# Edge counts of a graph network stored as bfloat16 instead of bytes, and fed to TensorE without a cast

## The reference, cut to what matters

```
# layer 2, a polynomial of degree 5 in the normalised adjacency
for k in range(1, 6):
    tx = segment_sum(norm[:, None] * tx[col], row, num_segments=N)    # norm = dis[row] * dis[col]
    result = result + coeffs[k] * tx
# layer 3, two graph convolutions
h = x @ W
agg = segment_sum(h[src] * (dinv[src] * dinv[dst])[:, None], dst, num_segments=N)
out = agg + h / deg[:, None] + b
```

## Time and profile before

| what | value |
|---|---|
| median of 3 runs | 7933.46 us (7933.38 to 7944.13) |
| profiled execution, its own time | 7934.18 us |
| its span, first to last instruction | 7932.5 us |
| mean granted TensorE clock | 0.964 of full speed |
| busy | PE 6931.4 us (87%), DVE 5980.0 (75%), ACT 4364.6 (55%), POOL 2865.0 (36%) |
| DMA | 1425.59 MB, mean 180 GB/s |
| casts of counts, ACT L1384 | 500 in the polynomial, mean 1475 ns; 200 in the convolutions, mean 1475 ns |
| casts of counts, DVE L1468 | 500, mean 1033 ns; 200, mean 1022 ns |

### The profile page before, as it was taken

One profiled execution on the slowest core, in us unless ns is written; L12 is line 12 of the kernel. 1 busy time (PEld: TensorE's weight loads), 2 busy tenths in 40 slices (PEclk: granted clock), 3 DMA queues, 4 the chain that ended last, 5 costly groups with the idle time before them and its releaser, 6 DMA issues. The chain is left out here.

```text
span 7932.5 us, 279512 instructions
## 1 busy us (share of the span) xinstructions
PE 6931.4 (87%) x98699; PEld 5909.3 (74%) x98724; DVE 5980.0 (75%) x17395; ACT 4364.6 (55%) x13164; POOL 2865.0 (36%) x2957
## 2 busy tenths in 40 slices
PE   2799999999999799999994888888895999998888
PEld 1455555555555599999994787788895998997878
DVE  4567776777767599898996799799898667776556
ACT  0122222222222299999994787787795666665555
POOL 0588888888878655454552000000000000000000
PEclk9999999999999999999997999999998999998889
DMA  9522222222222277676674887887895777764645
GB/s 391 164 59 60 59 61 60 59 59 60 59 60 59 64 230 232 227 230 230 229 231 156 284 298 278 284 298 280 297 334 191 200 201 201 201 195 133 175 136 162
DMA packets 656939, 1425.59 MB, mean 180 GB/s; under 512 B 284864, under 2 KB 352190, under 8 KB 653265
## 3 DMA queue, kind: packets, MB, share of 16 engines
q1 hardware_dynamic: 540674, 1232.57, 48.4%
q0 software_dynamic: 101792, 92.82, 5.6%
q10 hardware_dynamic: 13924, 93.06, 3.1%
HBM read 982.95 MB, written 433.34 MB: 179 GB/s over the span
## 5 line engine op out<-in xcount | busy, mean ns | idle before, releaser
L340 POOL DMA_INDIRECT sorted_rows<-sort_rows,sort_row_at x1600 | 1979.4, 1237 | 579.2 <-issue 565.2
L1603 ACT ACTIVATE smooth_msg<-smooth_ps_a,smooth_w_rows 128x64 f32<-128x64 f32 x6000 | 1311.9, 334 | 315.7 <-PE smooth_ps_a L1689 299.2
L371 ACT ACTIVATE sort_count<-sort_ps_c 50x50 bf16<-50x50 f32 x1600 | 331.7, 207 | 1903.2 <-PE sort_ps_c L403 1903.1
L1384 ACT ACTIVATE poly_cast<-poly_mat 128x1536 bf16<-128x1536 uint8 x500 | 714.8, 1475 | 445.0 <-PE poly_ps L1405 370.2
L399 PEld LDWEIGHTS sort_ps_r<-sort_count,sort_hot_dt 50*125 50x125 bf16 x1600 | 282.7, 177 | 837.1 <-issue 582.4
L413 PE MATMUL sort_ps_m<-sort_w,sort_hidden 128*125 128x64 f32 x3200 | 879.3, 430 | 0.0
L1711 PE MATMUL smooth_ps_s<-smooth_msg,smooth_hot 128*128 128x64 bf16 x7500 | 773.9, 195 | 76.2 <-DVE smooth_last_part L1842 65.4
L392 PE MATMUL sort_ps_h<-sort_attrs,sort_w 24*128 24x500 f32 x800 | 811.6, 1115 | 18.1 <-DMA sort_attrs<-in_attr_t 18.1
L1711 PE MATMUL smooth_ps_s<-smooth_rest,smooth_hot 128*128 128x64 bf16 x7500 | 769.8, 194 | 16.0 <-issue 15.9
L1711 PE MATMUL smooth_ps_s<-smooth_last_part,smooth_hot 128*128 128x64 bf16 x7500 | 768.9, 194 | 16.1 <-issue 16.1
L413 PEld LDWEIGHTS sort_ps_m<-sort_w,sort_hidden 128*125 128x125 f32 x3200 | 732.1, 320 | 41.1
(11 more groups left out here) (332 smaller groups left out, 16527.5 us busy)
## 6 DMA issues: line engine op xcount, KB each, us to landing
poly_mat<-counts_t SPq DMA_DIRECT2D x500, 400.0 KB, 3.7
smooth_src<-src_rows SPq DMA_DIRECT2D x150, 960.0 KB, 5.0
smooth_hot<-hot_rows SPq DMA_DIRECT2D x150, 960.0 KB, 7.0
smooth_src<-src_rows SPq DMA_DIRECT2D x150, 640.0 KB, 5.7
smooth_hot<-hot_rows SPq DMA_DIRECT2D x150, 640.0 KB, 6.9
graph_edges<-sorted_rows SPq DMA_DIRECT2D x125, 700.0 KB
hot_rows<-graph_hot SPq DMA_DIRECT2D x125, 640.0 KB, 3.6
src_rows<-graph_hot_t SPq DMA_DIRECT2D x125, 640.0 KB, 3.4
```

Of the source, the lines that this page charges most:

```text
L340: pool.indirect_dma_start(out=sorted_rows, out_offset=bass.IndirectOffsetOnAxis(row_at[u][:, j:j + 1], 0), in_=rows[u][:, j, :], in_offset ...
L1384: act.activation(cast[u][h][:, DVE_S:HR, :], mat[u][h][:, DVE_S:HR, :], ACT.Copy)\
L1603: last = act.activation(at[:, i, :], ps_a[g % 2][:, i * D:(i + 1) * D], ACT.Copy, scale=w_rows[u][:, c * CHUNK + i:c * CHUNK + i + 1])
```

## The change

`st_c`, `st_t`, `counts` and `counts_t` become bfloat16, so the stores of counts and the loads of `mat` carry twice the bytes (a half of a row is 800 KB). The `cast` tiles, ACT's and DVE's casts and their semaphores go. PE reads `mat` itself and waits for the load's semaphore. SP reloads the first half of a row when PE has done 25 blocks of the row two before it (`half_done`, new), the second when PE has done the row (`row_done`). So two rows of `mat` are all that lies between DRAM and PE. ACT has only `write_table` left in `spread`.

```diff
-        st_c = [sb(f"st_c{b}", [128, 2, S_LOAD, 128], U8) for b in two]
-        st_t = [sb(f"st_t{b}", [128, S_LOAD, 2, 128], U8) for b in two]
+        st_c = [sb(f"st_c{b}", [128, 2, S_LOAD, 128], BF16) for b in two]
+        st_t = [sb(f"st_t{b}", [128, S_LOAD, 2, 128], BF16) for b in two]
...
-        mat = [[sb(f"mat{u}{h}", [128, HR, 128], U8) for h in two] for u in two]
-        cast = [[sb(f"cast{u}{h}", [128, HR, 128], BF16) for h in two] for u in two]
+        mat = [[sb(f"mat{u}{h}", [128, HR, 128], BF16) for h in two] for u in two]
...
-        cast_v, cast_a, row_done, row_kept = (sem(n) for n in ("cast_v", "cast_a", "row_done", "row_kept"))
+        row_done, row_kept = sem("row_done"), sem("row_kept")
+        half_done = sem("half_done")
...
-                                for by in (cast_a, cast_v):
-                                    sp.wait_ge(by, 2 * number(k, p, u) + (h + 1 - 4))
-                                    sp.sem_inc(taken, 1)
+                                sp.wait_ge((half_done, row_done)[h], number(k, p, u) - 1)
+                                sp.sem_inc(taken, 1)
...
-                def pair(k, p):
-                    for u in two:
-                        if not at_start(k, p):
-                            act.wait_ge(row_done, number(k, p, u) - 1)
-                        for h in two:
-                            act.wait_ge(loaded[u][h], k * 16 * PAIRS + 16 * p + 16)
-                            act.activation(cast[u][h][:, DVE_S:HR, :], mat[u][h][:, DVE_S:HR, :], ACT.Copy)\
-                               .then_inc(cast_a, 1)
-
                 for k in range(n_passes):
-                    pair(k, 0)
                     act.wait_ge(posted, PAIRS * (k + 1))
                     spilled.write_table(act, xs)
-                    with act.Fori(1, PAIRS) as p:
-                        pair(k, p)
...
                         if b in (0, HR):
-                            for by in (cast_a, cast_v):
-                                pe.wait_ge(by, 2 * number(k, p, u) + (b // HR + 1))
+                            pe.wait_ge(loaded[u][b // HR], k * 16 * PAIRS + 16 * p + 16)
...
-                        last = nc.tensor.matmul(ps[u][:, 0:3 * D], cast[u][b // HR][0:NL, b % HR, :],
+                        last = nc.tensor.matmul(ps[u][:, 0:3 * D], mat[u][b // HR][0:NL, b % HR, :],
                                                 parts[k % 2][:, b].rearrange("p i d -> p (i d)"),
                                                 start=b == 0, stop=b == NB - 1 and not own_edges)
+                        if b == HR - 1:
+                            last.then_inc(half_done, 1)
...
-                def cast_half(k, p, u, h):
-                    dve.wait_ge(loaded[u][h], k * 16 * PAIRS + 16 * p + 16)
-                    dve.tensor_copy(cast[u][h][:, 0:DVE_S, :], mat[u][h][:, 0:DVE_S, :]).then_inc(cast_v, 1)
-
...
-    counts = dram("counts", [NB, 128, NB, 128], U8)
-    counts_t = dram("counts_t", [NB, 128, NB, 128], U8)
+    counts = dram("counts", [NB, 128, NB, 128], BF16)
+    counts_t = dram("counts_t", [NB, 128, NB, 128], BF16)
```

More of the change, by code:

```diff
@@ L1322, in spread @@
     HR = NB // 2
-    DVE_S = 13
     SPILL_AT, LATE, TWICE = 2, 6, 20
@@ L1476, in pair @@
                         for h in two:
[L1477 to L1480, removed]
                             by_row[u].go(at_once)
@@ L1485, in pair @@
                     ahead.end()
-                for u in two:
-                    for h in two:
-                        cast_half(0, 0, u, h)
                 none = Beside(iter(()))
```

## The result

The changed kernel takes 8103.7 us (median of 4 runs, 8092.5 to 8117.1) where the kernel before, run beside it, takes 7933.4. The ratio is 1.0213, interval 1.0192 to 1.0233: 170 us slower. The forecast was 7934 us, its range ended at 8020. The profiled execution has a span of 8115.4 us, 183 more than the one before. build_graph ends 16 us later than before (it takes 20 us more and starts 4 earlier), the polynomial takes 123 us more (1265.6 for 1142.2), the two convolutions 22 and 24; the parts between them give 3 back.

What follows compares the result with a forecast made beforehand. PE was taken to be full in the steady parts, with DMA loads the new limit (397 GB/s asked, 404 expected). The terms, -17.6 - 14.7 + 1.6 + 11.4 + 14 + 5 = -0.3 us, gave 7934 us, range 7895 to 8020.

Steps and rivals of the forecast that it cites:

- Term 5: Steady rows of spread: PE's rate stays, loads nearly keep up; 2 us lost a pass, +14 us (0 to +114).
- Term 1: Four seams between passes: waits for DVE's posts and ACT's cast go, a 2.6 us load stall comes; -17.6 us.
- Term 2: Spilled edges, seven times: DVE's chain starts 1.6 us earlier without its casts, 0.5 for the clock; -14.7 us.
- Term 3: Three stage starts: waits for DVE's and ACT's casts go, row 2's late half comes; +0.55 us each, +1.6 us.
- Term 4: y_sb's load and the zero fill share the engines with the rows' loads, so PE stalls more; +11.4 us (-38 to +50).
- Term 6: build_graph: stores of counts double, mostly into idle queue time, DVE's edge loads behind them; +5 us (0 to +100).
- Rival B: In spread the DMA engines become the bound, a full share being only 368 GB/s: about 8065 us; chance 0.27.
- Rival A: Loads keep up, Terms 4 to 6 are nil, the shorter DVE chain is net gain: -31 us, 7903 us; chance 0.22.
- Rival C: In build_graph the edges' load slips behind the longer stores: +75 us, 8009 us; chance 0.10.
- Rival D: The change doesn't do what it says, PE still gated by something of the casts' pace: 7934 us; chance 0.03.

Runs made afterwards that it cites:

- dtype_only: The kernel before with counts, their tiles and mat in bfloat16, the casts kept as copies to cast: 8009.1 us, ratio 1.0095.
- depth4: The changed kernel with four rows of mat instead of two: 7971.3 us, ratio 1.0046 to the kernel before.
- few_mm: The changed kernel with PE multiplying only 12 of the 50 blocks of a row, all loads as they are: 7923.6 us, single run.
- graph_only: The kernel before with bfloat16 counts in build_graph alone, spread loading and casting as many bytes as before: 7952.7 us, ratio 1.0017.
- half4: The changed kernel with four rows of mat and, after each stage's first loads, 13 of 25 blocks loaded per half row: 7868.4 us, ratio 0.9919.
- late8_act: depth4 with spilled edges after pair 3, earlier pairs' steps from pair 8, two pairs' from 18, y_sb's load on ACT's queue: 8019.2 us, ratio 1.0107.
- store_twice: The kernel before with build_graph storing each group's counts a second time, as bytes, into tensors nobody reads: 7942.8 us, ratio 1.0014.

## Why the prediction was wrong, point by point

The steps from the kernel before to the changed one, each measured to some 15 us: the type, +75 us (dtype_only); the casts out, with four rows of room kept, -38 us (depth4); four rows of room made two, +132 us.

- **Term 5, the step that failed.** "At 404 or 416 GB/s nothing is lost ... I take 2 us a pass." The rate of the engines was read rightly: 400 to 405 with more room, 417 in few_mm. What was wrong is to take it for the rate of this loop. Three halves under way and 6.4 us to landing allow 384 GB/s at most, and with the signalling it is 369. A row takes 4.45 us, 0.325 us more than before. Over the 44 rows of a pass behind the spilled edges this is 14.3 us, 100 us in seven passes (114 if all 50 rows went at this pace), where the sum had 2 us a pass, 14 in all. The prediction had pieces for it: it put the landing of an 800 KB load at 4.7 us, a lone load into an idle queue (the quickest of the 500 took 4.3), and used that at the seam only. In a steady loop the load stands behind two others; and "four halves in flight" counted the one in PE's hands.
- **Term 1, seams.** The wait for DVE's posts and ACT's cast went, and row 2's second half became late, as put. But it is 4.68 us late (4.4 to 6.5 at the four seams) in place of 2.6, with 0.92 and 0.74 us for the loads around it. The 300 matmuls take 0.9 us more than before, not 4.4 less. In depth4, where no load is late, they take 7.8 us less.
- **Term 2, spilled edges.** Right: PE is away 3.65 us (6441.55 to 6445.20), 3.9 were named.
- **Term 3, stage starts.** The wait fell from 23.96 to 23.05 us, as put; the first 300 matmuls take 32.3 us where 29.3 stood. About +2 us each, not +0.55.
- **Term 4, y_sb and zeros.** Direction right, size too small: 5.3 to 9.1 us for the longest stall of a pass where 4 were named, then a wait of some 1.2 us at each half while the zeros are written. From the spilled edges to the next pass 2200 matmuls take 213.8 us where 192.0 stood (6445.20 to 6658.95; 6403.64 to 6595.65). Of these 21.8 us the steady rate explains 14.3 (44 rows x 0.325); the other 7.5 go with the foreign traffic and the slower clock behind its stalls, and the sum had 0.9.
- **Term 6, build_graph.** +5 was taken. build_graph takes 20 us more in the changed kernel's profile and 15 in graph_only's, whose ratio gives 13. The share rose to 0.81 (about 0.85 was named) and ACT's copies kept their time, as put; DVE's late edges did not grow (22 waits, 13.1 us, where the earlier trace rows has 26, 16.3). The mechanism named was not the one: PE's small waits grew, for ACT at L825 from 9.1 to 14.2 us, at L805 and L806 together from 0.7 to 9.8.
- **Rival B** named the right place, the right pace (4.45 us a row) and nearly the right total, 8065. Its reason was wrong: a full share is not 368 GB/s. That its total came near is partly luck, for it kept the 31 us that terms 1 to 3 were to win, and of these the changed kernel shows almost nothing. The Trainium skill's 358 GB/s ("DMA: Bandwidth & Descriptors", section "Where 436 GB/s comes from") is not the bound here: this core's loads ran at 405 GB/s over 100 us in depth4.
- **Rival A** is half4's world: with bytes as before and four rows, 7868. It went 35 us below A's 7903, since the stalls at y_sb went too. A's price of DVE's release, -31 us, is near the -38 between dtype_only and depth4; that two such sums agree to 7 us is partly luck, since this step also moved the room from `cast` to `mat`. **Rival C** falls by the count of edges above. **Rival D** falls: ACT is gone from PE's waits, and DVE is left with the start of the stages, the spilled edges and ten waits of at most 0.6 us for its sums.

## What to carry to other kernels

A stage between a load and its use may be two things: work, and room. Before taking it out, count what lies under way without it: the bytes that can be in flight (not those in the consumer's hands) over the landing time under load bound the rate of the loop, and this has to exceed the consumer's, whatever the engines can do (here 384 GB/s against 397). With no more SBUF, cut the buffers into smaller pieces and release each as it is used. And when loads fill the engines, look at every other transfer in the loop; its delay moved from wait to wait here as the schedule gave it more rows, and where the engines had more to do behind it (the zero fill) more rows won nothing.

## What the runs showed of the hardware

- **The DMA share does not measure the rate.** It is 0.98 at 369 GB/s, 1.01 at 405, 1.02 at 417, with the same 6400-byte packets (mean 270 ns in the changed kernel, 254 in depth4, 249 in few_mm). A share near 1 is no proof that the engines are the bound.
- **y_sb's load slows the rows' packets.** While its packets of 12,800 bytes run beside the rows' of 6400, the engines are full and move 251 to 257 GB/s (late8_act). In the changed kernel's pass 1 (6207.6 to 6219.0) the rows' packets take 417 ns on average where 270 stood, y_sb's 916; in late8_act, on ACT's queue, 409 and 780. No run loads y_sb with nothing beside it, so what its packets would take alone is not shown.
- **More stores, fewer matmuls.** A DMA share of 0.89 instead of 0.70 in build_graph (store_twice) took 0.5% of the matmuls. PE's groups kept their mean times; what grew was idle time for which the profile shows no releaser, from 0.3 to 9.1 us.
- **ACT's copies go by elements.** 1475 ns from bytes and 1481 from bfloat16 (1536 elements, dtype_only). DVE's of 1664 elements fell from 1033 to 597 ns.
